# One transpose of the rough maxima ahead of the norm's, and the guard rows ahead of the query's high half

## What is computed

```python
def _L1_xattn_ref(query, key, value, Wq, bq, Wk, bk, Wv, bv, Wo, bo):
    # NUM_KV = 8 heads, GROUPS = 4, HEAD_DIM = 16
    Q = query @ Wq + bq
    K = key @ Wk + bk
    V = value @ Wv + bv
    ...
    scores = jnp.einsum('bhgqd,bhkd->bhgqk', Q, K) * scale
    w = jax.nn.softmax(scores, axis=-1)
    y = jnp.einsum('bhgqk,bhkd->bhgqd', w, V)
    ...
    return y @ Wo + bo
x = x + _L0_xattn_ref(_layernorm(x, axis=-1), ctx_4096, ctx_4096)
x = x + _L0_ffn_ref(_layernorm(x, axis=-1), ...)
x = x + _L1_xattn_ref(_layernorm(x, axis=-1), ctx_4096, ctx_4096, ...)
x = x + _L1_ffn_ref(_layernorm(x, axis=-1), ...)
```

## Time and profile before

| what | value |
|---|---|
| median of 3 runs | 731.49 us (730.99 to 735.34) |
| profiled execution, its own time | 727.8 us |
| its span | 726.0 us |
| PE busy | 675.9 us, 93%, 3952 matmuls |
| ACT busy | 503.2 us, 69% |
| DVE busy | 494.6 us, 68% |
| POOL busy | 382.3 us, 53% |
| granted TensorE clock, mean | 0.990 |

### The profile page before, as it was taken

The page is one execution under the profiler, slowest core; times in us unless marked ns, Lnnn a source line. Parts: engine busy times, 40 slices in busy tenths (PEclk is TensorE's granted clock), DMA queues, the critical chain, the costliest instruction groups (busy, mean ns, idle before and its releaser), DMA issues.

```text
span 726.0 us, 12481 instructions
## 1 busy us (share of the span) xinstructions
PE 675.9 (93%) x3952; PEld 488.6 (67%) x3952; DVE 494.6 (68%) x1125; ACT 503.2 (69%) x901; POOL 382.3 (53%) x465
## 2 busy tenths in 40 slices
PE   8689999999878988899999999999999999998894
PEld 3345555655454666677887787877878877876672
DVE  4787888878724857676776776776777767757412
ACT  3577878767525978778678688688697786785210
POOL 1558999987753134254554652652553554544433
PEclk9999999999998999999999999999999999999998
DMA  7234344353212310110110101101101101000000
GB/s 249 89 104 136 124 147 131 116 160 92 83 59 92 95 50 1 45 44 16 59 35 25 45 16 55 43 14 58 43 14 58 43 14 58 14 16 29 1 15 29
DMA packets 25783, 45.71 MB, mean 63 GB/s; under 512 B 3184, under 2 KB 4976, under 8 KB 25744
## 3 DMA queue, kind: packets, MB, share of 16 engines
q1 hardware_dynamic: 25744, 45.24, 19.7%
HBM read 36.84 MB, written 8.39 MB: 62 GB/s over the span
## 4 chain that ended last, share of the span: by engine, by line
PE 51%; ACT 16%; DVE 11%; issue 11%; POOL 10%; POOLq 0%; DVEq 0%; ACTq 0%
ACT x L422 6%; PE ps_b L1011 5%; ACT q_stack L422 5%; PE ps_b L1013 5%; PE ps_b L1012 5%; PE bank L1079 4%; PE ps_b L1049 4%; PE ps_a L1049 4%; PE wide L1011 4%; PE wide L1069 4%; PE wide L1013 3%; PE wide L1012 3%; POOL x_res L711 3%; DVE x_in L768 2%; POOL stage L688 2%
## 5 line engine op out<-in xcount | busy, mean ns | idle before, releaser
L422 ACT ACTIVATE q_stack<-qt_h 32x512 fp32r<-32x512 f32 x128 | 80.7, 630 | 1.9
L618 POOL TENSOR_TENSOR va<-mv,small 128x1 f32<-128x1 f32 x80 | 15.4, 192 | 124.1 <-DVE mv L991 78.6
L708 POOL TENSOR_TENSOR y_l<-y,y_h 128x512 fp32r<-128x512 f32 x16 | 20.6, 1290 | 110.4 <-ACT y_h L560 110.4
L1011 PE MATMUL ps_b<-down_h,ht_h 128*128 128x512 f32 x128 | 53.4, 418 | 3.4 <-DVE ht_l L955 2.7
L920 DVE RECIPROCAL y<-ps_b 128x256 f32<-128x256 f32 x32 | 55.9, 1748 | 0.0
L1011 PE MATMUL wide<-up_h,t_h 128*128 128x512 f32 x128 | 52.3, 408 | 1.2 <-DVE t_l L900 1.2
L1013 PE MATMUL wide<-up_h,t_l 128*128 128x512 f32 x128 | 50.7, 396 | 0.0
L1012 PE MATMUL wide<-up_l,t_h 128*128 128x512 f32 x128 | 50.6, 395 | 0.0
L1013 PE MATMUL ps_b<-down_h,ht_l 128*128 128x512 f32 x128 | 50.6, 395 | 0.0
L1012 PE MATMUL ps_b<-down_l,ht_h 128*128 128x512 f32 x128 | 50.5, 394 | 0.0
L620 POOL TENSOR_TENSOR rs<-va,small 128x1 f32<-128x1 f32 x80 | 44.0, 550 | 6.3
(11 more groups left out here) (203 smaller groups left out, 2180.4 us busy)
## 6 DMA issues: line engine op xcount, KB each, us to landing
x_in<-in_x SPq DMA_DIRECT2D x16, 256.0 KB, 2.7
ctx_t<-in_ctx SPq DMA_DIRECT2D x16, 256.0 KB, 2.6
x_res<-in_x SPq DMA_DIRECT2D x16, 256.0 KB, 2.6
x_in<-x_rows SPq DMA_DIRECT2D x16, 256.0 KB, 2.6
ctx_t<-in_ctx_turned SPq DMA_DIRECT2D x16, 256.0 KB, 2.9
x_res<-x_rows SPq DMA_DIRECT2D x16, 256.0 KB, 3.5
out<-stage SPq DMA_DIRECT2D x16, 256.0 KB, 2.0
x_rows<-x SPq DMA_DIRECT2D x8, 256.0 KB, 2.1
```

Source lines behind the costliest of these rows:

```text
L422: last = act.activation(out[STACK * part:STACK * (part + 1), p, :], halves[STACK * p:STACK * (p + 1), :].bitcast(F32), ACT.Copy)
L1011: pe.matmul(out_ps, w_hi, m_hi, start=start, stop=False)
```

## The change

The maxima of a tile are now kept as one 128 x 128 array: 2 batches x 2 halves of the query groups x 32 columns, of which 8 are used and 24 stay zero (DVE clears gmax once, at the start of pass 2). One transpose turns them all, where four turned eight columns each. The maxima of the four parts then lie in rows 0, 32, 64 and 96 and the seven rows after each, in 128 columns. ACT again makes four copies, now one for each part, each of which repeats its 128 columns for the four pairs. The transpose stands ahead of the norm's transposes on PE (these are now `turned_norm`), and the guard copies stand ahead of `query_high` on ACT.

```diff
-        gmax = sb("gmax", [P, 2, 2, 2, PART])
+        gmax = sb("gmax", [P, 2, 2, STACK])
...
-                query_high(i + 4)
                 t = i + 3
                 if live(t):
                     act.wait_ge(S["gmt_ps"], t + 1)
                     wait(act, S["s_ps"], 2 * t)
                     act.wait_ge(S["sel_s"], 3)
-                    for p in range(PAIRS):
-                        last = act.activation(q_stack[GUARD:GUARD + NKV, p, :], bank[1][0:NKV, :],
-                                              ACT.Copy, scale=-1.0)
+                    guards = q_stack[GUARD:GUARD + NKV].rearrange("h p (g b q) -> h p g b q", g=GROUPS, b=2)
+                    for b in range(2):
+                        for n in range(2):
+                            quarter = bank[1][STACK * (2 * b + n):STACK * (2 * b + n) + NKV, 0:P]
+                            last = act.activation(guards[:, :, 2 * n:2 * n + 2, b, :],
+                                                  quarter.rearrange("h (g q) -> h g q", g=2).unsqueeze(1)
+                                                  .to_broadcast([NKV, PAIRS, 2, SEQ]), ACT.Copy, scale=-1.0)
                     last.then_inc(S["ngm_s"], 1)
+                query_high(i + 4)
+                t = i + 3
+                if live(t):
...
+            dve.memset(gmax[:], 0.0).then_inc(S["vbd_zero"], 1)
...
-                    dve.tensor_reduce(gmax[:, b, :, r, :],
+                    dve.tensor_reduce(gmax[:, b, :, PART * r:PART * (r + 1)],
...
                     last.then_inc(S["kv_ps"], 1)
+
+            def turned_norm(t):
+                if live(t):
                     pe.wait_ge(S["xn3_s"], t + 1)
                     wait(pe, S["ht_lo"], 2 * (t - 3))
                     for c in range(DC):
...
                 if early(i):
                     keys_values(0)
+                    turned_norm(0)
...
                     pe.wait_ge(S["gmax_s"], 4 * t + 4)
-                    turned = bank[1][0:NKV].rearrange("h (g b q) -> h b g q", g=GROUPS, b=2)
-                    for b in range(2):
-                        for n in range(2):
-                            last = pe.transpose(turned[:, b, 2 * n:2 * n + 2, :],
-                                                gmax[:, b, n].rearrange("p r h -> p (r h)"), ident)
-                    last.then_inc(S["gmt_ps"], 1)
+                    pe.transpose(bank[1][:, 0:P], gmax[:].rearrange("p b n h -> p (b n h)"), ident).then_inc(S["gmt_ps"], 1)
+                turned_norm(i + 4)
```

More of the change, by code:

```diff
@@ L873, in _ @@
             dve.memset(vbd[:], 0.0).then_inc(S["vbd_zero"], 1)
+            dve.memset(gmax[:], 0.0).then_inc(S["vbd_zero"], 1)
             dve.memset(zero_col[:], 0.0).then_inc(S["vbd_zero"], 1)
-            dve.wait_ge(S["vbd_zero"], 2)
+            dve.wait_ge(S["vbd_zero"], 3)
             def merged(c):
```

## The result

The changed kernel takes 738.65 us (median of 12 runs, 737.01 to 744.43), the kernel before beside it 731.69 (12 runs, 727.66 to 736.76): a ratio of 1.0099, 95% interval 1.0071 to 1.0127, so 5.2 to 9.3 us slower. The forecast was 728.4 with a range of 726.3 to 732.6. The profiled execution took 738.61, its span is 736.8 us, 10.8 more than the one shown of before.

What follows compares the result with a forecast made beforehand. PE's queue was taken to bound full tiles: 0.33 us saved less 0.03 stall, times twelve tiles, gives -3.6; the opening adds 0.5, so -3.1 from 731.49 to 728.4 us, range 726.3 to 732.6.

Steps and rivals of the forecast that it cites:

- What bounds the kernel: Second pass, full tiles: PE's queue sets 28.16 us per tile; time removed from x3 to the queries' end isn't given back.
- PE's saving: PE, second pass: one transpose of the maxima for four, 0.34 us instead of 0.67, saving 0.33 us per tile.
- the ACT term: ACT, ahead of x_h: the four new guard copies take 2.02 us, as the old four did.
- the other end: ACT guard copies: upper cost of 0.63 us each without overlap, 2.54 together, from 32x512 copies out of SBUF.
- Rival (a): ACT guard copies dearer, 2.54 us: queries +0.13 per tile, opening 2.1, sum +3.7, 735.2, slower; chance 0.08.
- The stall: PE at the start of the queries, waiting for x_l behind x_h: 0 to 0.09 us per tile, taken as 0.03.
- the opening: Tiles 0 to 2 of the second pass, bound by the copies: +0.48, +0.37 and -0.35, together +0.50 us.
- the forecast's 0.48 and 0.37: Opening tiles 0 and 1: query products start later, at 244.25 instead of 243.77 and 269.05 instead of 268.68.
- The range: Whole kernel: 726.3 to 732.6 us, leaving out Rival (a) and the ends of the medians' spread.

Runs made afterwards that it cites:

- The last kernel: Changed kernel with guard copies shared: two on ACT ahead of x_h, one behind, the fourth on DVE; 731.50 beside 732.45, or 727.45 with idle matmuls in PE's waits.
- the one from the same rows: Changed kernel with all four guard copies reading rows 0 to 7 of the bank (result not the reference's); 734.94 beside 733.46, ratio 1.0025.
- The order-alone kernel: Kernel before, its own four transposes moved ahead of the norm's and its four old guard copies ahead of the query's high half; 738.91 beside 731.51, ratio 1.0095.
- the filled pair: Kernel before and changed kernel, each with two idle matmuls in each of PE's first three waits of the first pass; 730.81 and 736.77 beside 733.46.
- the filled kernel before: Kernel before with two idle matmuls of zeros in each of PE's first three waits of the first pass; 730.81 beside 733.46, ratio 0.9988.
- two variants: Changed kernel with x_h between the second and third guard copy, 736.02; changed kernel with one transpose but both old orders, 741.50; each beside 731.51.

## Why the prediction was wrong

**What bounds the kernel** held: PE's queue sets the full tile, and time taken out between x3 and the queries' end isn't given back at x3. The last kernel shows it, with 0.31 us of the 0.33, and so does the one from the same rows, with 0.26.

**PE's saving** held: 0.32 measured for 0.33.

**The step that failed first is the ACT term**, "I take 2.02, as that is the nearest row". It is 2.39, and it turned the full tiles from a gain to a loss: 340.0 us for the twelve with it, 335.4 with 2.02, 338.6 before. The row was the nearest by count and source, but not by the source's place: its four copies read one group of rows, the new ones read four. I had kept 2.54 as the other end, from the 32x512 copies out of SBUF, and called SBUF the difference. Rival (a) was the right mechanism for the full tiles, an x_l that comes too late behind dearer copies, with too little chance (0.08).

**The stall was undersized beyond that.** With 2.39 my own sum gives a stall of 0.31 and a tile of 28.15; measured are 0.36 of lateness and 0.10 for the fresh start behind it. The step "a stall of 0 to 0.09" took a handover that ends just in time as free. The order-alone kernel shows that it costs about 0.1 even with a lead of 0.14. The forecast of 0.03 for this stall stands against 0.36 + 0.10.

**The second step that failed is the opening**, forecast at +0.5 from the distances of the copies alone. With 0.37 us more per tile it would be +1.6; measured +3.2 (tiles 0 to 1 +0.86, 1 to 2 +0.88, 2 to 3 +1.45). The first two are the forecast's 0.48 and 0.37, each plus 0.37, and 0.14 more in the second. Of the third, 1.3 goes with the lower clock, for which the prediction had no term. This step would have failed with the right ACT term too: with copies of 2.02 the opening is still 3.6 above before, 2.4 of it from tile 2 to tile 3. So even then there would have been no gain to measure (734.94 beside 733.46).

**The rest isn't settled.** From tile 0 to the end the changed kernel takes 4.7 us more in the first pair of profiled executions (522.6 and 517.9), 4.7 in the second (522.4 and 517.8) and 6.3 in the filled pair. Of the last, 1.3 are in the stretch behind tile 15, which took 89.7 in the filled kernel before and 88.1 in the unfilled ones with the same instructions, so it moves by itself. The medians differ by 7.0 (5.2 to 9.3), the filled ones by 6.0. The first pass can't have been made slower by its own instructions, which are the same, and its start scatters by 5 us in before. With 8 in 83 for a start as in the profile shown, 18 runs of the changed kernel miss it about one time in six, so that none had it can be chance. But chance and the 4.7 us together don't make the whole difference: 39 of the 83 runs of before lie below 732.3, and with 4.7 us added they would lie below 737.0, where not one of the 18 lies. Between the medians one to two us are left that the traces behind tile 0 don't show. Whether the changed kernel gets a good start less often, or loses more behind it in the runs without a trace, these runs can't tell.

**The range** failed with the rest: it left out the slow side, where a mechanism of mine already stood at 735.2, and the measured median lies above that one too. The lucky start isn't part of this miss, as the forecast was taken off the median of before (731.49), and the median beside the result is 731.69.

## What to carry to other kernels

When an edit changes which partitions consecutive instructions read, its cost isn't in the row of the old ones, even where count, shape and engine agree: look for a row in which that changes too. A cover isn't free down to its last tenth: here a lead of 0.04 us from ACT on PE cost 0.30, one of 0.14 from DVE cost 0.09 and one of 0.28 from DVE nothing. Where two results share one engine, giving a small piece to an engine with room gave back in the full tile what reordering only moved. Compare first the stretch that the edit doesn't touch: here it held more than half of the difference between the two traces.

## What the hardware showed that I had not expected

- Consecutive ACT copies out of PSUM overlapped by 0.09 us while they read the same eight rows (4 in 2.02), and not at all when each read another group of rows (4 in 2.39), with a strided destination as with a plain one. The Trainium skill (ScalarE: Activation LUTs, What ACT_TABLE_LOAD costs) says that back-to-back ACTIVATEs overlap by about 93 ns; the trace agrees for the first kind only.
- From the end of an ACT copy to the PE matmul that needs it, 0.25 us in the loop (534.32 to 534.57), 0.14 from DVE (532.18 to 532.32), and then 0.1 more until the second matmul.
- The same program had its tile 0 at 208.09 and at 213.14 us, with a granted clock of 1.00 and of 0.52 between 15 and 20 us; with six idle matmuls in PE's first three waits it was 1.00 there in all three traces.
- The granted clock of ten microseconds fell to 0.83 in the opening of the changed kernel and to 0.66 in two variants (300 to 310 us), and stayed at 1.00 between 290 and 310 in three traces of the kernel before.
